# First expert of the last layer from slot tables, x loaded behind the context, key row in three bf16 parts

## What is computed

```
# attention of layers 0 and 3 (one head, 256 wide); layer 0 has a mask and key bias
scores = (layernorm(x) Wq + bq) (ctx Wk + bk)^T / 16 ;  x += tanh(g) * softmax(scores) (ctx Wv + bv) [Wo + bo]

# feed-forward of layer 3: top-1 gate, 8 experts, capacity C = 2048 / 8 = 256
gates = softmax(x2d @ wg); idx = argmax(gates); mask = one_hot(idx, E)
loc = cumsum(mask, axis=0) - 1;  mask = mask * (loc < C)      # a token over capacity is dropped
di[e, loc] = x2d of the tokens of expert e                    # "dispatch"
h = relu(einsum('ecm,emh->ech', di, w1)); eo = einsum('ech,ehm->ecm', h, w2)
out[token] = gate * eo[e, loc];  x += tanh(g) * out
```

## Time and profile before

| | us |
|---|---|
| three timed runs | 891.32, 892.33, 895.99 (median 892.33) |
| profiled execution | 897.07 |
| its span | 895.3 |
| PE busy | 855.6 (96% of the span) |
| DVE / ACT / POOL busy | 461.7 / 326.6 / 210.3 |
| first layer's attention begins (first keys) | 16.01 |
| last layer's experts begin | 774.78 |
| last product ends | 888.6 |

### The profile page before, as it was taken

The page is one execution under the profiler, slowest core; times in us unless marked ns, Lnnn a source line. Parts: engine busy times, 40 slices in busy tenths (PEclk is TensorE's granted clock), DMA queues, the critical chain, the costliest instruction groups (busy, mean ns, idle before and its releaser), DMA issues.

```text
span 895.3 us, 15721 instructions
## 1 busy us (share of the span) xinstructions
PE 855.6 (96%) x6100; PEld 669.5 (75%) x6108; DVE 461.7 (52%) x1240; ACT 326.6 (36%) x628; POOL 210.3 (23%) x241
## 2 busy tenths in 40 slices
PE   8999999999999998889999999988999999999997
PEld 7776665678888876667777777755777779988886
DVE  2773676500132306577777777766998786000000
ACT  2434122112322222555555645646554441112121
POOL 1121233020434310000100101114665116112212
PEclk9997999999999999899999999999999999999999
DMA  7031911014746338000000000000000012336451
GB/s 238 25 130 36 303 76 50 25 53 165 231 156 198 112 95 300 1 2 1 2 2 1 2 1 1 2 1 1 2 1 2 30 42 91 125 115 201 146 167 22
DMA packets 33877, 70.64 MB, mean 79 GB/s; under 512 B 9218, under 2 KB 23946, under 8 KB 28939
## 3 DMA queue, kind: packets, MB, share of 16 engines
q1 hardware_dynamic: 26937, 59.92, 18.8%
q0 software_dynamic: 6144, 8.31, 4.8%
q10 hardware_dynamic: 722, 1.39, 0.4%
HBM read 54.98 MB, written 14.80 MB: 78 GB/s over the span
## 4 chain that ended last, share of the span: by engine, by line
PE 88%; DVE 6%; ACT 3%; issue 2%; DVEq 1%; POOL 0%; POOLq 0%; ACTq 0%
PE banks L618 80%; DVE small L2018 2%; PE banks L1127 2%; PE banks L1206 1%; ACT arena L1308 1%; PE banks L954 1%; PE banks L1141 1%; ACT arena L1360 1%; PE banks L714 1%; PE banks L1020 1%; ACT arena L1489 1%; PE banks L1165 1%; ACT arena L1504 0%; DVE arena L2058 0%; DVE small L1647 0%
## 5 line engine op out<-in xcount | busy, mean ns | idle before, releaser
L618 PE MATMUL banks<-arena 32*120 32x256 f32 (+6 forms) x1808 | 160.1, 378 | 7.2 <-DVE small L2018 4.2
L1308 ACT ACTIVATE arena<-banks 128x512 f32<-128x512 f32 (+4 forms) x185 | 106.8, 597 | 163.1 <-PE banks L1091 34.3
L618 PEld LDWEIGHTS banks<-arena 32*120 32x120 f32 (+5 forms) x1808 | 99.6, 164 | 38.4 <-issue 19.0
L618 PE MATMUL banks<-ffw,arena 128*128 128x256 bf16 (+2 forms) x632 | 116.7, 338 | 0.5 <-issue 0.2
L618 PE MATMUL banks<-arena,ew 128*128 128x256 f32 x512 | 113.3, 379 | 1.4 <-ACT arena L1308 1.4
L618 PE MATMUL banks<-ew,arena 128*128 128x256 f32 x512 | 113.2, 379 | 0.0
L618 PEld LDWEIGHTS banks<-arena,ew 128*128 128x128 f32 x512 | 97.1, 190 | 15.0 <-ACT arena L1308 1.8
L618 PEld LDWEIGHTS banks<-ew,arena 128*128 128x128 f32 x512 | 96.2, 190 | 12.5
L618 PEld LDWEIGHTS banks<-ffw,arena 128*128 128x128 f16 (+1 forms) x640 | 84.5, 135 | 23.8 <-issue 2.4
L2018 DVE TENSOR_REDUCE small<-banks 128x16 f32<-128x1920 f32 x32 | 69.1, 2158 | 23.6 <-PE banks L618 23.6
L1965 DVE TENSOR_SCALAR arena<-banks,arena 128x256 f32<-128x256 f32 x16 | 7.1, 479 | 120.7 <-PE banks L618 120.7
(11 more groups left out here) (244 smaller groups left out, 1309.8 us busy)
## 6 DMA issues: line engine op xcount, KB each, us to landing
ew<-in_w SPq DMA_DIRECT2D x32, 1024.0 KB, 7.2
xrow<-arena SPq DMA_DIRECT2D x1, 2064.0 KB, 20.9
arena<-xrow SPq DMA_DIRECT2D x8, 258.0 KB, 4.3
zrow<-arena SPq DMA_DIRECT2D x8, 256.0 KB, 2.2
ffw<-in_shared SPq DMA_DIRECT2D x2, 1024.0 KB, 6.4
acc<-x SPq DMA_DIRECT2D x4, 512.0 KB, 3.5
ffw<-in_tern SPq DMA_DIRECT2D x2, 1024.0 KB, 8.2
out<-x SPq DMA_DIRECT2D x8, 256.0 KB, 2.0
```

The costliest lines, as they stand in the source:

```text
L618: return pe.matmul(o, l, r, start=a, stop=b)
L1308: return nc.scalar.activation(o, i_, ACT.Copy)
```

## The change

1. **Start.** 7 of the first 15 fillers, 2 of the next 4 and all 12 before the first keys are gone. The q0 column has its own bank and is made before the folded product; DVE reads it before it normalizes the first rows. ACT issues tg and the mask ahead of the context; SP waits for the context before it issues the rest of x and all that follows.
2. **Key row of layer 3.** During units 8 to 10 of the stream POOL splits krow into three bf16 parts (key_part), and SP copies each into a partition of browT. The scores of layer 3 begin with one bf16 product with K = 3.
3. **Last layer's first expert.** EARLY is 10: tiles 0 to 9 are moved as before; then SP reads the 256 columns of expert 0's slots. Late tiles 10 to 15 come to expert 0 by products with tables late[:, t - 10, slot] (1 where the token has the slot, among slots 0 to 255), four made by POOL, two by DVE; the rows read are added by a product with the identity. Only behind the read of expert 0 does POOL move tiles 10 to 15, and SP then reads experts 1 to 7 and expert 0's two other columns. Expert 1's transposes stand inside the second product of expert 0. The 62 fillers before the experts are gone, and 2, 3 and 3 of others in the gate loop.

```diff
-FILL = {0: {0: 6}, 3: {5: 8, 6: 14, 7: 18}}
+FILL = {0: {0: 6}, 3: {5: 6, 6: 14, 7: 15}}
+EARLY = 2 * GROUPS[1][1]
...
+        c.at = 15360
+        kpart = c.take(NB * SK, dt=BF16)
+        c.at = 18906
+        late = c.take(6 * CAP, "p (i n) -> p i n", i=6)
+        slot256 = Mf[:, 0, :]
...
+            sp.wait_ge(load["ctx"], 16)
             sp.dma_start(x[:, 4:, :], d["x"][:, 4:, :]).then_inc(load["x"], 16)
...
+            for p in range(3):
+                sp.wait_ge(su["parts"], p + 2)
+                sp.dma_start(browT[p:p + 1, 0, :], kpart[0:1, :]).then_inc(load["parts"], 16)
...
-            sp.wait_ge(gt["moved"], 16 * NT)
+            sp.wait_ge(gt["moved"], 16 * EARLY)
             rows_of = xrow[0:T, :].rearrange("(e t p) n -> p e t n", p=P, t=TB)
-            for e in range(E):
-                sp.dma_start(G3[:, e, :, :], rows_of[:, e, :, :]).then_inc(ex["rows" if e else "rows0"], 16)
+            sp.dma_start(G3[:, 0, :, 0:D], rows_of[:, 0, :, 0:D]).then_inc(ex["rows0"], 16)
+            sp.wait_ge(ex["gather2"], 64 + 16 * (NT - EARLY))
+            sp.dma_start(G3[:, 1, :, :], rows_of[:, 1, :, :]).then_inc(ex["blank"], 16)
+            for e in range(2, E):
+                sp.dma_start(G3[:, e, :, :], rows_of[:, e, :, :]).then_inc(ex["rows"], 16)
+            sp.dma_start(G3[:, 0, :, D:], rows_of[:, 0, :, D:]).then_inc(ex["rows"], 16)
...
-                    for n, (a, b) in enumerate(GROUPS[1:]):
-                        g.wait_ge(gt["slot"], n + 2)
-                        for t in range(2 * a, 2 * b):
-                            move(t)
+                    g.wait_ge(gt["slot"], 2)
+                    for t in range(2 * GROUPS[1][0], EARLY):
+                        move(t)
+                    g.wait_ge(gt["slot"], 3)
+                    for t in range(EARLY, NT - 2):
+                        g.tensor_scalar(late[:, t - EARLY, :], slot256, slotf[:, t:t + 1], None, ALU.is_equal)
+                    g.drain().then_inc(su["consts"], 1)
+                    g.wait_ge(ex["rows0"], 16)
+                    for t in range(EARLY, NT - 2):
+                        move(t)
+                    g.wait_ge(gt["slot"], 5)
+                    for t in range(NT - 2, NT):
+                        move(t)
...
+                def key_part(p):
+                    if p == 0:
+                        g.wait_ge(su["krow"], 2)
+                        g.wait_ge(multi["s_ps"], 2 * NB)
+                    else:
+                        g.wait_ge(load["parts"], 16 * (p + 1))
+                    g.tensor_copy(kpart[0:1, :], krow[0:1, :])
+                    g.drain().then_inc(su["parts"], 1)
+                    if p < 2:
+                        g.tensor_tensor(krow[0:1, :], krow[0:1, :], kpart[0:1, :], ALU.subtract)
+                        g.drain()
...
-            fill(psum[7], 15)
+            fill(psum[7], 8)
...
-            fill(psum[7], 4)
+            fill(psum[7], 2)
...
+            column(psum[7][:, 0:KC], WT[:, 1], COL["q0"]).then_inc(su["col_ps"], 1)
             product(psum[4], WT[:, 1], WT[:, 0]).then_inc(su["B_ps"], 1)
             column(psum[5][:, 0:KC], WT[:, 0], COL["k0"])
-            column(psum[5][:, KC:2 * KC], WT[:, 1], COL["q0"])
...
-                    mm(o, onesf[0:1, :], bcast(krow[0:1, k * SK:(k + 1) * SK], 1, TB), True, False)
+                    if L == 0:
+                        mm(o, onesf[0:1, :], bcast(krow[0:1, k * SK:(k + 1) * SK], 1, TB), True, False)
+                    else:
+                        mm(o, ones[0:3, :], bcast(browT[0:3, 0, k * SK:(k + 1) * SK], 1, TB), True, False)
...
                     if L == 0:
-                        fill(psum[7], 12)
...
                         group_ranks(3)
-                        fill(psum[3], 40)
-                        pe.wait_ge(gt["moved"], 16 * NT)
-                        fill(psum[3], 22)
...
+                def prepare_first():
+                    def by_slots(t):
+                        for k in range(KC):
+                            m = mm(MISC[k][:, 0:CAP], zx[:, t, k * P:(k + 1) * P], late[:, t - EARLY, :], t == EARLY, t == NT - 1)
+                        return m
+                    pe.wait_ge(su["consts"], 2)
+                    for t in range(EARLY, NT - 2):
+                        by_slots(t)
+                    pe.wait_ge(q["rows0"], 16)
+                    for k in range(KC):
+                        for t in range(TB):
+                            mm(MISC[k][:, t * P:(t + 1) * P], G3[:, 0, t, k * P:(k + 1) * P], ident[:, :], False, False)
+                    pe.wait_ge(gt["slot"], 4)
+                    for t in range(NT - 2, NT):
+                        m = by_slots(t)
+                    m.then_inc(q["xT_ps"], 1)
...
-            act.dma_start(ctxT[:, :, :], d["ctxT"]).then_inc(load["ctx"], 16)
             act.dma_start(tg[:, :], d["g"].partition_broadcast(P)).then_inc(load["tiny"], 16)
             act.dma_start(m0_i[0:1, :], d["m0"]).then_inc(load["tiny"], 16)
+            act.dma_start(ctxT[:, :, :], d["ctxT"]).then_inc(load["ctx"], 16)
...
+                    if n == 3:
+                        for t in range(t0, t1):
+                            m = V.tensor_scalar(late[:, t - EARLY, :], slot256, slotf[:, t:t + 1], None, ALU.is_equal)
+                        m.then_inc(gt["slot"], 1)
```

More of the change, by code:

```diff
@@ L422, in move @@
                 g.indirect_dma_start(xrow, bass.IndirectOffsetOnAxis(ap=slot_i[:, t:t + 1], axis=0), zx[:, t, :], None)\
-                 .then_inc(gt["moved"], 16)
+                 .then_inc(gt["moved"] if t < EARLY else ex["gather2"], 16)
             def one_gate(L):
@@ L573, in stream @@
                         rstd_of(s + 2)
+                    if NB <= s < NB + 3:
+                        key_part(s - NB)
+                    elif s == NB + 3:
+                        g.wait_ge(load["parts"], 16 * 4)
                     if s >= NB + 4:
@@ L598, in _ @@
             g.tensor_copy(zx.bitcast(I32)[:, :, D], token_i)
+            s16 = slot256.rearrange("p (a b) -> p a b", a=16)
+            g.tensor_scalar(s16, bcast(iota16[:, :], 2, 16), 16.0, None, ALU.mult)
+            g.drain()
+            g.tensor_tensor(s16, s16, bcast(iota16[:, :], 1, 16), ALU.add)
             g.drain()
@@ L943, in prepare @@
                         pe.wait_ge(q[f"gather{n % 3}"], 32 * (n // 3 + 1))
-                    elif b == 0 and u == 0:
-                        pe.wait_ge(q["rows0"], 16)
+                    elif n == 1:
+                        pe.wait_ge(q["blank"], 32)
                     else:
@@ L968, in first, with second @@
                             m.then_inc(q["h_ps"], 1)
-                def second(i, u):
+                def second(i, u, between=lambda: None):
                     if i * 2 + u >= 2:
@@ L977, in second @@
                         for k in range(MC):
+                            if t and k == 4:
+                                between()
                             if t == 0:
@@ L992, in experts @@
                         mm(psum[7][:, 0:2], onesf[:, :], gam[:, 0:2], True, True).then_inc(su["gsum_ps"], 1)
+                    if L == 3 and n == 0:
+                        second(b + BASE[L], u, lambda: prepare(BASE[3], 0, 1))
+                        continue
                     if n + 1 < E:
@@ L1380, in main @@
                     if L == 0:
-                        act.wait_ge(su["col_sb"], 1)
+                        act.wait_ge(su["col_sb"], 2)
                         take_k(0)
@@ L1425, in _ @@
             copy(W["v0"][:, :, :], psum[0].rearrange("p (m n) -> p m n", m=KC)).then_inc(su["B_sb"], 1)
-            act.wait_ge(su["col_ps"], 2)
+            act.wait_ge(su["col_ps"], 3)
             copy(wkb, psum[1][:, 256:256 + KC])
@@ L1435, in take_rows @@
                     copy(xeT[:, u], MISC[u][:, :].rearrange("p (k n) -> p k n", k=KC)).then_inc(q["xT_sb"], 1)
-                take_rows(BASE[L], 0)
+                if L == 0:
+                    take_rows(BASE[L], 0)
+                else:
+                    act.wait_ge(q["xT_ps"], E + 1)
+                    copy(xeT[:, 0], banks[:, 6 * 512:8 * 512].rearrange("p (k n) -> p k n", k=KC)[:, :, 0:CAP]).then_inc(q["xT_sb"], 1)
                 for n in range(E):
@@ L1952, in last_moe @@
                 q = ex
[L1953 removed]
+                v.wait_ge(q["blank"], 32)
                 v.wait_ge(q["rows"], 16 * (E - 1))
```

19 lines of the change are left out of this document (12 added, 7 removed).

## The result

| | before | after |
|---|---|---|
| median of 16 timed runs, us | 892.36 (891.29 to 900.30) | 881.75 (881.26 to 890.47) |
| ratio | | 0.9885, 95% interval 0.9861 to 0.9909 |
| profiled execution | 897.07 | 890.32 |
| its span | 895.3 | 888.5 |
| first keys | 16.01 | 11.69 |

The kernel became 10.6 us faster; 880.4 was forecast, range 875.5 to 886.5. The profiled execution of the changed kernel is one of its two longest: 890.32 at a mean granted clock of 0.981, where nine of the 16 took 881.3 to 881.8 at 0.993 to 0.995. Four runs at 0.991 took 884.0 to 884.3. So the profile shows more low clock than the median run had: it has three stretches of 3.4 us at 0.50 that the profile of before has not, from 18.7, from 704.8 and from 759.4. At half speed they cost up to 1.7 us each, 5.1 together, which is about what lies between the 885.1 forecast for the profiled execution and its 890.32.

A forecast was written before the change was run, and what follows sets the result against it. TensorE's chain of waits, 88% of the span, was taken to bound the kernel. Start 3.9, key row 2.25 and first expert 5.8 sum to 11.95 us off 892.33, giving 880.4 us, range 875.5 to 886.5.

The forecast's parts named there:

- Start: Kernel start: fewer fillers, earlier column and reordered loads bring first keys from 16.01 to 12.0; 3.9 us, bounds 1.1 to 4.6.
- One condition: At the start: the context, issued at 1.7, lands at 8.9 and is needed only at 10.9.
- The cover argument for x: At the start: x, issued later but alone, needs half its 12.1 us, in time for DVE at 19.2; otherwise 2.8 lost.
- Key row: Layer 3's attention loop: one bf16 product replaces a float32 pair, 0.45 us in five of eight batches; 2.25, bounds 1.2 to 3.2.
- First expert: Last layer's hand-over: table products for late tiles start the first expert at 769.0, not 774.78; 5.8 us, bounds 3.5 to 8.0.
- the hand-over from POOL: Before the last experts: after POOL's four tables, 3.75 us from 758.07, PE starts at 762.0 with the hand-over, 0.2 forecast.
- The two loads that come next: During expert 0: expert 1's rows have 4.8 us of slack; all rows land by 781, wanted at 784; both hidden.
- The tables' price, 0.937: Last layer's hand-over: each POOL slot table of 128x256 costs 0.937 us, four 3.75; the skill's rule gave 0.38 to 0.55.
- Sum: Whole kernel: 3.9 + 2.25 + 5.8 = 11.95 us saved, giving 880.4 timed and 885.1 profiled.
- the clock falls in the new gap: Rival, before the last experts: PE's 2.4 us without work drops its clock; +3 us, 883.4; chance 0.17.
- The forecast's own sign of being wrong: Before the last experts: granted clock at 0.50 in PE's new gap, where the forecast expected 1.00.
- The first loop's clock: Rival, first layer's loop: its low-clock stretch may vanish (874) or double (887); chance 0.10, a half each way.

The follow-up runs named there:

- c0_before: The kernel before, unchanged, profiled on the third chip, where the kernel before took 896.77 and 898.38 us in two sets.
- c1_after: The changed kernel, unaltered, run again on the third chip: 883.69 us against 896.77 for the kernel before, ratio 0.985.
- s11: s9b without SP's wait for the context before loading the rest of x: 885.95 us, ratio 0.9845 to the kernel before.
- s9b: Second run of the changed kernel with the four slot tables made by VectorE instead of POOL: 880.90 us, ratio 0.9787 to the kernel before.
- s7: The changed kernel with each of POOL's four slot tables made twice: 885.98 us, 2.3 above c1_after.
- s3: The kernel before with only the change to the last layer's first expert: 889.68 us, ratio 0.9898, on the second chip.
- s1: The kernel before with only the changed start: 894.16 us, ratio 0.9943, on the second chip.
- s2: The kernel before with only the key row in three bf16 parts: 896.95 us, ratio 0.9994, on the second chip.

## Why the prediction was right, step by step

- **Start, 3.9.** 4.06 between c0_before and c1_after, both at the full clock there. Transposes, key row and first keys came about 0.3 us or less from the forecast times, x in 7.5 us in place of 12.1, in time. One condition was misread: the context was taken as issued at 1.7 and landed at 8.9, 2 us before it was needed, while the change puts tg and the mask ahead of it. It went out at 2.80, landed at 10.7 and just held the key row, by 0.2 us. In the first comparison's profile only 2.58 were left at mark 1, since the clock was low from 19 to 22. The cover argument for x was sound, and s11 gives the price of the other order: 5.1, more than the whole gain of the start, 2.9 of it waits for loads. The Trainium skill, "DMA: Bandwidth & Descriptors", section "Queues, rings and completion order", has each DMA engine take packets in turn from the queues with work. The trace agrees, though it would look the same if the queues shared in another way: on ACT's queue the context took 9.7 us and the 128 KB of the bias row behind it 12.1 beside x (s11), and 7.8 and 7.8 ahead of x (s9b).
- **Key row, 2.25.** 1.97 between the key rows at the full clock, five steps at 0.39 to 0.40 each, as many as forecast; the 0.45 was a touch high. That the clock can fall in the step where PE's wait grew, 1.64 us in half of the profiles, the prediction had not seen.
- **First expert, 5.8.** 3.46 in the first comparison's profile (22.01 to 18.55). The missing 2.3 is the clock, 1.7 (16 instructions in 5.32 and not 3.62), and the hand-over from POOL, 0.7 (0.93 to the end of its drain and not 0.2), less 0.1 on the tables. The mis-sized term was this hand-over. At the full clock the part is 5.2. The two loads that come next were hidden, as said. A slip in the working changed nothing: from 762.5 the last of six moves starts five spacings of 1.265 later, at 768.8, and not six.
- **The tables' price, 0.937.** 0.92 measured, and s7 shows that it counts in full. The Trainium skill, "GPSIMD Engine Reference", section "Elementwise — side-by-side cycle accounting", gives an estimated 0.38 to 0.55; the trace does not agree, and the row of the same shape was the better guide.
- **Sum.** At the full clock 4.06 + 1.97 + 5.2 = 11.2, against 11.95; the medians give 10.6. The 0.6 between is of the size of low stretches that only some runs have. Two are known: 1.64 us in the third step of the last loop, and the rival "the clock falls in the new gap" (+3 forecast, 1.7 in that profile, 3.0 in c1_after). The forecast's own sign of being wrong, the granted clock at 0.50 in that gap, did show, if only from 759.4, at the gap's very end. All four profiles with POOL's tables and no fillers (after, s3, c1, s7) have a low stretch there. But c0, s1 and s2 have one near there too, with the old hand-over and without the gap, and in s3, c1 and s7 PE also waits for DVE ahead of the last ranks, so the gap is not shown as the cause. The median lies between the forecast's 880.4 and its 883.4. How often the clock falls in the timed runs can't be read from them, and that so little of it is in the median is luck: the sum had nothing for it.
- **The first loop's clock.** Both lengths occur (50.5 and 56.0) with the old start and with the new one: c0_before and s1 have the long stretch, s2 and c1_after have not. So no effect of the change is seen there, and the difference is one from run to run.
- **What the prediction had not seen**: it took the hand-over of before as one number, 22.0. On two other chips it is 26.4 to 27.9, and on the third the gain is 13.1 in place of 10.6. The three parts alone gave 4.6, 1.8 and 9.1 us on the second.

The version with VectorE's tables beats the kernel before twice, and the changed kernel in the set that had both: 0.979 (0.9757 to 0.9818) against 0.985 (0.982 to 0.988).

## What to carry to other kernels

Price a step that stands alone on the path by the row of its own shape and engine, then ask whether an idle engine does it in a third of the time: here it was 3.7 us of POOL against 1.1 of DVE. Cut spans at marks before comparing profiles; a part whose length changes from run to run of one kernel must be taken out first. Where a saved piece of work only lengthens a wait, look at the clock behind that wait. Fillers pay only if they end before the work they cover, at the low clock too.

## What the runs showed of the hardware that was not expected

- In all 14 profiles a stretch at the low clock lasted 3.4, 6.8, 10.3 or 13.7 us (the one at the very end of each left out), at different places in runs of one kernel. One of 3.4 us made a step of the last loop 1.64 us longer (9.15 and 7.52), one of 13.7 us made marks 1-2 5.5 us longer.
- It fell behind an idle time of 1.14 us (18.72, after), and did not behind 1.15 in the same place in c1_after.
- A subtraction of 1x960 on POOL takes 2.00 us, as long as 128x1024: here the length of a row counts, not the partitions.
- PE starts 0.93 to 0.94 us after the end of POOL's tables (after, c1_after), when POOL's drain ends, but 0.10 after the second set of them in s7; ACT's copy releases it within 0.1 us.
- The same kernel's TensorE and VectorE stood still for 1.2 and 4.5 us at one place on two chips (c0_before, and near the same in s1 and s2, which have the same hand-over), and not in the first comparison.
